# Expert rows weighted on chip and added to x1 in DRAM by accumulating scatters

## What is computed

```python
# layer 1: token mixing with a decaying scan over time, then residual and layer norm
xk, xv, xr = (x * m + shifted(x) * (1 - m) for m in (mix_k, mix_v, mix_r))
k, v, r = xk @ Wk.T, xv @ Wv.T, xr @ Wr.T
x1 = layernorm(x + (sigmoid(r) * wkv(decay, first, k, v)) @ Wo.T)

# layer 2: 8 experts, the best two of each token
logits = x1 @ Wg + bg
topk_scores, topk_idx = top_k(logits, 2)
topk_scores = softmax(topk_scores)
h = x1 @ W1[e] + b1[e];  a = gelu(h) if e is even else silu(h)
y[e] = a @ W2[e] + b2[e]
out = layernorm(x1 + sum over the two experts of topk_scores * y[e])
```

## Time and profile before

| | us |
|---|---|
| median of 3 runs (733.85 to 735.19) | 734.34 |
| the profiled execution, its own time | 729.4 |
| its span, first to last instruction | 727.4 |

### The profile page before, as it was taken

One profiled execution on the slowest core, in us unless ns is written; L12 is line 12 of the kernel. 1 busy time (PEld: TensorE's weight loads), 2 busy tenths in 40 slices (PEclk: granted clock), 3 DMA queues, 4 the chain that ended last, 5 costly groups with the idle time before them and its releaser, 6 DMA issues.

```text
span 727.4 us, 14812 instructions
## 1 busy us (share of the span) xinstructions
PE 639.8 (88%) x4525; PEld 591.6 (81%) x4525; DVE 461.5 (63%) x963; ACT 392.5 (54%) x715; POOL 304.7 (42%) x353
## 2 busy tenths in 40 slices
PE   8999999999876789999999999999999999996000
PEld 5887878878654689999999999999999999996000
DVE  4869999999996485574554654455534543432694
ACT  3576587568742244563636364665645455551474
POOL 5111044744665673191461722542821821112363
PEclk9999999999987799999999999999999999999555
DMA  8510232232317648514151142141231121100893
GB/s 258 135 30 15 73 110 96 86 102 81 108 60 232 197 153 277 184 51 151 37 167 40 43 161 61 35 161 51 76 131 41 29 60 46 31 28 32 285 299 117
DMA packets 57116, 78.75 MB, mean 108 GB/s; under 512 B 5190, under 2 KB 46611, under 8 KB 56884
## 3 DMA queue, kind: packets, MB, share of 16 engines
q1 hardware_dynamic: 41540, 51.59, 22.1%
q0 software_dynamic: 6496, 16.99, 6.6%
q10 hardware_dynamic: 8976, 8.72, 4.5%
HBM read 49.14 MB, written 28.92 MB: 107 GB/s over the span
## 4 chain that ended last, share of the span: by engine, by line
PE 72%; DVE 9%; issue 6%; POOL 4%; ACT 3%; DMA 3%; another core or an unknown queue 1%; SPq 0%; ACTq 0%; DVEq 0%; POOLq 0%
PE hT_ps L897 28%; PE y_ps L906 26%; PE vr_ps L734 6%; PE k_ps L734 5%; PE xT_ps L915 2%; PE wo_ps L742 2%; POOL records_dram L639 2%; DVE o_all L1245 1%; PE small_ps L756 1%; DMA recs<-records_dram 1%; PE xT_ps L725 1%; POOL rstd_c L693 1%; PE xT_ps L804 1%; ACT res L1163 1%
## 5 line engine op out<-in xcount | busy, mean ns | idle before, releaser
L897 PE MATMUL hT_ps<-xTh,wx 128*128 128x256 f32 x1120 | 212.3, 287 | 2.1 <-DVE aTl L1217 1.4
L906 PE MATMUL y_ps<-wx,aTh 128*128 128x256 f32 x1088 | 197.5, 283 | 1.1 <-DVE y_sb L1231 1.1
L897 PEld LDWEIGHTS hT_ps<-xTh,wx 128*128 128x128 f32 x1120 | 178.7, 193 | 2.8 <-DVE aTl L1217 1.6
L906 PEld LDWEIGHTS y_ps<-wx,aTh 128*128 128x128 f32 x1088 | 169.7, 192 | 1.3 <-issue 1.3
L674 POOL DMA_INDIRECT expert_out_dram<-y_sb,dest x70 | 68.3, 975 | 243.0 <-DVE y_sb L1231 227.4
L1217 DVE TENSOR_TENSOR aTl<-hT_ps,aTh 128x512 fp32r<-128x512 f32 x140 | 93.1, 688 | 118.0 <-ACT aTh L1108 114.6
L897 PE MATMUL hT_ps<-xTl,wx 128*128 128x256 f32 x560 | 159.3, 285 | 0.0
L906 PE MATMUL y_ps<-wx,aTl 128*128 128x256 f32 x544 | 154.0, 283 | 0.0
L1102 ACT ACT_TABLE_LOAD x33 | 42.3, 1283 | 170.3 <-PE hT_ps L897 163.4
L1102 ACT ACTIVATE hT_ps<-hT_ps,b_c 128x256 f32<-128x256 f32 x280 | 113.4, 467 | 20.0 <-DVE dest L1210 13.1
L897 PEld LDWEIGHTS hT_ps<-xTl,wx 128*128 128x128 f32 x560 | 108.5, 194 | 0.0
(11 more groups left out here) (201 smaller groups left out, 860.0 us busy)
## 6 DMA issues: line engine op xcount, KB each, us to landing
staging<-in_L_ffn_W SPq DMA_DIRECT2D x16, 1024.0 KB
recs<-records_dram ACTq DMA_DIRECT2D x33, 258.0 KB, 2.8
yy<-expert_out_dram SPq DMA_DIRECT2D x16, 512.0 KB, 5.5
xin<-in_L_attn_x SPq DMA_DIRECT2D x16, 256.0 KB, 4.4
xres<-in_L_attn_x SPq DMA_DIRECT2D x16, 256.0 KB, 3.2
x_dram<-rec SPq DMA_DIRECT2D x16, 256.0 KB
xx<-x_dram SPq DMA_DIRECT2D x2, 2048.0 KB
out<-res SPq DMA_DIRECT2D x16, 256.0 KB, 4.2
```

The source lines that it names most:

```text
L897: ins = pe.matmul(hT_ps[b][:, f, :], wx[:, s, part, off:off + P], xpart[t.slot % 2][:, cc, :], start=k == 0, stop=k == len(terms) - 1)
L906: ins = pe.matmul(y_ps[h], apart[t.slot % 2][:, fc, h * P:(h + 1) * P], wx[:, s, part, off:off + C], start=k == 0, stop=k == len(terms) - 1)
```

## The change

Each expert row is weighted on chip before it leaves, and added to its token's x1 row in DRAM. No separate tensor of expert rows exists any more.

- **Weights in the chunks.** `choose` writes the difference of the two scores (`gap`) in place of the copy `top2`. A new ACT function `weigh(c)` makes both weights, sigmoid(-gap) and sigmoid(gap), in columns C+3 and C+4 of the record. It stands before `exponents(i)` for chunk i-3 in the steps 3 to 7, and later for the last three chunks (after `normalise_x1(6)`, before `normalise_x1(7)`, and at the very end). The record now has 261 words instead of 258: x1, token number, both slots, both weights. The whole score calculation between the stages is gone. POOL's `send_records` also waits for `weigh`.
- **Blocks.** The row number is now the token number. `halves` no longer computes it; a new DVE function `mark` copies it and finds each record's weight in four small instructions, and stands after `lower_parts`. `outputs` adds the bias in place in PSUM, waits, then multiplies by the weight into `y_sb`: two instructions for each half in place of one.
- **Scatters.** POOL's indirect DMA writes into `x1_dram` with `compute_op=ALU.add`. Before the first half of block t it waits until both scatters of block t-1 have landed.
- **Last stage.** `xx`, `yy`, `y2`, `res` and their loads and sums are gone. SP issues eight loads (`zz`), each four tokens to a partition, 4 KB in one piece and 512 KB in all; DVE takes the statistics of four tiles, POOL makes four scales and shifts, ACT normalises in place, SP stores 512 KB.

The diff, cut to its core:

```diff
-    REC = C + 2
+    REC = C + 5
...
-    ys = nc.dram_tensor("expert_out_dram", (2 * TOKENS, C), F32, kind="Internal").ap()
+    sums = x1d.rearrange("b t c -> (b t) c")
...
-                if e == 2:
-                    for b in range(B):
-                        sp.dma_start(xx[:, :, b, :], x1d[b].rearrange("(q p) c -> p q c", p=P)).then_inc(xx_in, 16)
...
+            for g in range(GROUPS):
+                sp.dma_start(zz_of(g), rows_of(x1d, g)).then_inc(zz_in[g], 16)
+            for g in range(GROUPS):
+                sp.wait_ge(c_res, TILE * (g + 1))
+                sp.dma_start(rows_of(out, g), zz_of(g)).then_inc(res_out, 16)
...
+                pool.wait_ge(weighed, c.upto(2))
...
+                    previous = t - 1
                     for h in range(BH):
                         pool.wait_ge(y_done, t.upto(BH, h + 1))
+                        if h == 0 and previous.exists:
+                            pool.wait_ge(y_out[previous.slot], previous.turn(16 * BH, 16 * BH))
                         take_wait(pool)
                         pool.indirect_dma_start(
-                            ys, bass.IndirectOffsetOnAxis(ap=dest[t.slot][:, h:h + 1], axis=0), y_sb[t.slot][:, h, :], None,
-                            bounds_check=2 * TOKENS - 1, oob_is_err=False).then_inc(y_out[t.slot], 16)
+                            sums, bass.IndirectOffsetOnAxis(ap=dest[t.slot][:, h:h + 1], axis=0), y_sb[t.slot][:, h, :], None,
+                            bounds_check=TOKENS - 1, oob_is_err=False, compute_op=ALU.add).then_inc(y_out[t.slot], 16)
...
+            def weigh(c):
+                at = c.number % RECS
+                act.wait_ge(gap_done, c.upto(1))
+                scattered(act, c)
+                act.activation(rec[at][:, :, C + 3], gap[:], ACT.Sigmoid, scale=-1.0).then_inc(weighed, 1)
+                act.activation(rec[at][:, :, C + 4], gap[:], ACT.Sigmoid).then_inc(weighed, 1)
...
+                if (i - 3).exists and i.number < NCH:
+                    weigh(i - 3)
                 if i.exists:
                     exponents(i)
...
-            act.wait_ge(score_done, 1)
-            act.activation(score_t[:, :, 0:1], score_t[:, :, 0:1], ACT.Exp).then_inc(exp_done, 1)
...
+            for g in range(GROUPS):
+                act.wait_ge(c_rstd, g + 1)
+                for n in range(TILE):
+                    act.activation(zz_of(g)[:, n, :], zz_of(g)[:, n, :], ACT.Identity, bias=shift_c[:, g, n:n + 1],
+                                   scale=rstd_c[:, g, n:n + 1]).then_inc(c_res, 1)
...
+            def mark(u, own):
+                n = u.slot % 2
+                rows = recs[u.slot]
+                after(dve, y_out[u.slot], u.turn(16 * BH))
+                dve.tensor_copy(dest[u.slot][:], rows[:, :, C]).then_inc(dest_done, 1)
+                dve.tensor_tensor(hit[n][:], rows[:, :, C + 1:C + 3], own.rearrange("p a h -> p h a").broadcast_to([P, BH, 2]),
+                                  ALU.is_equal).then_inc(hit_done, 1)
...
+                dve.tensor_reduce(weight[u.slot][:], hit[n][:], AX.X, ALU.add).then_inc(weight_done, 1)
...
-                    dve.tensor_tensor(y_sb[u.slot][:, h, :], y_ps[h], b2_b[:, bass.ds(expert * C, C)],
-                                      ALU.add).then_inc(y_done, 1)
+                    dve.tensor_tensor(y_ps[h], y_ps[h], b2_b[:, bass.ds(expert * C, C)], ALU.add).then_inc(bias_added, 1)
+                    dve.wait_ge(bias_added, u.upto(BH, h + 1))
+                    dve.tensor_scalar(y_sb[u.slot][:, h, :], y_ps[h], weight[u.slot][:, h:h + 1], None, ALU.mult).then_inc(y_done, 1)
...
-                dve.tensor_copy(top2[:].rearrange("p i j k -> p (i j k)")[:, bass.ds(c.number * (2 * J), 2 * J)].rearrange(
-                    "p (j k) -> p j k", j=J), m8[:, :, 0:2]).then_inc(top2_done, 1)
+                after(dve, weighed, (c - 1).upto(2))
+                dve.tensor_tensor(gap[:], m8[:, :, 1], m8[:, :, 0], ALU.subtract).then_inc(gap_done, 1)
```

More of the change, by code:

```diff
@@ L204, in build @@
         m8 = sb("m8", [P, J, 8], F32, phase_a)
+        gap = sb("gap", [P, J], F32, phase_a)
         i8 = sb("i8", [P, J, 8], U32, phase_a)
@@ L254, in build @@
         dest = [sb(f"dest{n}", [P, BH], I32, phase_b) for n in range(RING)]
+        hit = [sb(f"hit{n}", [P, BH, 2], F32, phase_b) for n in range(2)]
+        weight = [sb(f"weight{n}", [P, BH], F32, phase_b) for n in range(RING)]
         xTh = [sb(f"xTh{n}", [P, CC, BLK], F32R, phase_b) for n in range(2)]
@@ L314, in build @@
         mm2_done, y_done = [sem(f"mm2_done{n}") for n in range(BH)], sem("y_done")
[L315 to L319, removed]
+        hit_done, weight_done, bias_added = sem("hit_done"), sem("weight_done"), sem("bias_added")
+        zz_in = [sem(f"zz_in{n}") for n in range(GROUPS)]
+        res_out = sem("res_out")
+        c_bn, c_mv, c_var, c_rstd, c_res = (sem(n) for n in ("c_bn", "c_mv", "c_var", "c_rstd", "c_res"))
         REC_DMAS = 2 * J * 16
@@ L355, in if_used, with rows_of, zz_of @@
             return eng.If(used > u.number) if u.largest >= ALWAYS else nullcontext()
[L357 to L368, removed]
+        def rows_of(ap, g):
+            b, q = g // (GROUPS // B), g % (GROUPS // B) * TILE
+            return ap[b].rearrange("(p q) c -> p q c", q=TILES)[:, q:q + TILE, :]
+        def zz_of(g):
+            b, q = g // (GROUPS // B), g % (GROUPS // B) * TILE
+            return zz[:, b, q:q + TILE, :]
         def after(eng, semaphore, value):
@@ L1491, in block_step @@
                         lower_parts(u)
+                u = t + 2
+                if u.exists:
+                    with if_used(dve, used, u):
+                        mark(u, own_f[:, bass.ds(u.number, 1)])
             blocks(dve, block_step)
-            dve.wait_ge(xx_in, 16 * B)
-            flat = score[:].rearrange("p n k -> p (n k)")
-            def first_sum(i):
-                dve.wait_ge(yy_in[i.slot], i.turn(16, 16))
-                after(dve, c_res, (i - RING).upto(B))
-                for b in range(B):
-                    dve.scalar_tensor_tensor(
-                        out=zz[i.slot][:, b, :], in0=yy[i.slot][:, b, 0:C], scalar=flat[:, bass.ds(column(i, b, 0), 1)],
-                        in1=xx[:, bass.ds(i.number, 1), b, :].rearrange("p a c -> p (a c)"),
-                        op0=ALU.mult, op1=ALU.add).then_inc(c_sum, 1)
@@ L1528, in out_step @@
-            def out_step(i):
-                for stage, c in ((first_sum, i), (statistics, i - 1), (second_sum, i), (means, i - 1)):
-                    if c.exists:
-                        stage(c)
-            pieces(dve, out_step)
-            last = Step(None, PIECES - 1, RING, PIECES)
-            statistics(last)
-            means(last)
+            for g in range(GROUPS):
+                dve.wait_ge(zz_in[g], 16)
+                for n in range(TILE):
+                    dve.bn_stats(stats_c[:, g, n, :], zz_of(g)[:, n, :]).then_inc(c_bn, 1)
+                dve.wait_ge(c_bn, TILE * (g + 1))
+                for n in range(TILE):
+                    dve.bn_aggr(mv_c[:, g, n, :], stats_c[:, g, n, :]).then_inc(c_mv, 1)
```

160 lines of the change are left out of this document (49 added, 111 removed).

## The result

| | before | after |
|---|---|---|
| median | 734.4 us (733.9 to 735.2) | 704.2 us (703.5 to 706.5) |
| profiled span | 727.4 us | 701.5 us |
| ratio | | 0.959 (95%: 0.957 to 0.962) |

What follows compares the result with a forecast made beforehand. It took DVE and PE, nearly full, to bound the chunks, PE the blocks, DMA with DVE the last stage. 7.3 + 1.0 + 1.5 - 22.2 = -12.4 us off 734.3 gave 721.9 us, range 711 to 733.

Steps and rivals of the forecast that it cites:

- Chunks, +7.3: Chunks: table loads for `weigh` delay the Exp on B by 3.1 us in steps 3 to 7, costing 7.3 us in sum.
- the loop: Chunks: dependence over two chunks, DVE to PE to ACT to DVE, as tight as DVE's own list; residual slack 2.2 us.
- Rivals 2 and 3: Chunks: table loads cost nothing, 714.6 us, 14%; or their full price in every chunk, 730.1 us, 12%.
- the drain: Chunks: the skill's 1.38 us added to each table switch, loop cost about 17 us, total near 731; chance 3%.
- Between the stages, 0: Between chunks and blocks: DVE's score instructions and the 4 MB load of x1 go, but PE waits for neither; nothing gained.
- Blocks, nothing: Blocks: added DVE work, about 1.5 us a block, and POOL's scatter waits fit beside PE's 11.94 us; no cost.
- Accumulating scatter, +1.5: End of the blocks: the last adding scatter lands later, 1.5 us, about half of an upper bound of 2.8.
- Rival 1: Blocks: the accumulating scatter becomes the bound; at 1 us a row about 934 us; chance 8%.
- Outputs, +1.0: End of the blocks: each output has one more instruction and wait, about 0.5 us, delaying PE's last product and the last scatter.
- Last stage, -22.2: Last stage: with half the loads it takes 31.2 us in place of 53.4, ACT setting the pace.
- Rival 4: Last stage: in-place tiles and 512 KB stores at the old pace leave 45 us or more, total 735 or above; 3%.
- From the span to the median, +4.9: Whole kernel: runs' median lay 4.9 us above the profiled execution; the same difference was assumed after the change.

Runs made afterwards that it cites:

- e4: Changed kernel with `weigh` of the first five chunks moved behind the upper halves, where Sigmoid is already loaded: 693.0 us, ratio 0.951 to the kernel before.
- e10: Changed kernel with `weigh` moved, operand distance 192, and `mark` of block 3 behind block 1's outputs: 692.8 us, ratio 0.944 to the kernel before.
- e1: Kernel before plus an unused 320-byte tile ahead of `recs`, giving the changed kernel's operand distance: 716.3 us, ratio 0.982.
- e3: Changed kernel plus two unused tiles restoring the operand places of the kernel before (distance 0): 711.9 us, ratio 0.976 to the kernel before.
- e5: Not the layer: only a block's products on constant operands, places swept in 32-byte steps; 48 first plus 48 second products took 10.90 to 11.52 us.
- e6: Changed kernel with plain scatters in place of accumulating ones (addition left out): 699.8 us, ratio 0.960 to the kernel before.
- e12: Kernel before plus an unused 192-byte tile ahead of `recs`, operand distance 192 in place of 0: 716.6 us, ratio 0.985.
- e2: Kernel before plus unused tiles of 1280 bytes ahead of staging and 320 ahead of `recs`, giving the changed kernel's operand places: 717.2 us, ratio 0.982.

## Why the prediction was right and wrong

- *Chunks, +7.3*: right in the mechanism, which e4 shows, since the loop was followed through both engines. That the sum agrees to the tenth is luck: chunk 7 cost 1.3 in place of 0.2, and chunks 4 and 6 each 0.5 less than worked out. Rivals 2 and 3 and the drain fall with it. What the prediction didn't ask is whether `weigh` could stand at a place in ACT's list where Sigmoid is loaded anyway; e4 shows that it can.
- *Between the stages, 0*: 1.8 us. e10 removes 1.3 of it: `mark` stands ahead of outputs for which PE waits in the first blocks, before the steady state whose slack the prediction used. The other 0.5 was not followed and is within what this stretch varies by.
- *Blocks, nothing*: here the step failed. The prediction went through DVE's and POOL's new work and found that PE waits for none of it, which is true from block 3 on. From that it put the stage at nothing, and so took the time of PE's own instructions as unchanged, for which it gave no reason. "The PE distance between blocks still 11.94" was the test set for it, and it read 11.55 to 11.75. e1 to e3 and e5 show the cause: the tiles moved by a few hundred bytes. That accounts for 9.2 of the 13.5 us by which the span was missed (10.2 to 10.7 us between like kernels at distances 0 and 64), and by the ratios of e1 and e3 for 12 to 13 us in the medians, 3 either way, of a miss of 18. This gain is luck: nothing in the idea of the change asks for it.
- *Accumulating scatter, +1.5*: mis-sized, 0.2 to 0.4 us by e6 and hidden by a shorter last group of products (5.74 against 6.02 us in the earlier trace rows). Half of an upper bound is no measurement. The Trainium skill ("Collectives: The Full Stack", The bandwidth ceiling) gives the halved pace of an adding transfer for large collectives in a ring. It is not seen in this scatter of 128 rows: 3.52 to 3.72 us with the addition against 3.32 without it in e6. Rival 1 falls.
- *Outputs, +1.0*: right, twice 0.5.
- *Last stage, -22.2*: -26.3. The mechanism was right up to the last store (ACT unbroken, 16 us). The wrong term is the tail, 3.8 us in place of 6.2 + 0.8: the 6.2 was taken for the time of a store, but the store landed after 2.1 and the end waited for POOL's DRAIN. By an estimate (727.4 - 723.3 before, 701.5 - 701.2 after) about 4 us of this stage's gain are that DRAIN, which no longer ends last, and not the lesser work. Rival 4 falls.
- *From the span to the median, +4.9*: the profiled execution of the kernel before lay 4.9 us below its median, and the prediction carried that over. After the change it was 0.7, so 4.2 us of the miss of 18 are this term. In which stage the slower executions lose them, no trace shows.
- *The range*: with every bound of the change's own terms it held the change at equal places (17 us, 15 to 20, so 717). It had no term for what it left untouched.

## What to carry to other kernels

A change in a tile's size or number moves every tile behind it, so compare the time of untouched instructions first (here 48 products, 5.75 us before and 5.46 or 5.66 after), and repeat the change once with padding that restores the old places before its gain is credited to its idea. Where PE is the bound, sweep the distance between its two operands in SBUF by itself; an unused tile of 128 to 320 bytes was worth 6 to 13 us here. Then time the kernel itself at the best places, for its own groups did not follow the sweep throughout (e12). And before the time behind a last store is called the store's, look for what ended last. An activation with another table should stand where that table is loaded anyway: in ACT's list, look for the last user of the same table ahead of the point where the value is needed.

## What the runs showed of the hardware that was not expected

- The pace of fp32r products of 256 columns depends on the distance modulo 256 bytes between the places of their two operands in SBUF: 48 of them take from 5.44 us (192) to 5.76 us (0), with nothing else running. The granted clock is 1.00 at either. The absolute place made no difference (wx moved by 1280 bytes from e1 to e2, by 32 in e5).
- An accumulating indirect scatter of 128 rows of 1 KB holds POOL for 1.55 us, the plain one for 0.98; its landing is 0.2 to 0.4 us longer (e6).
- POOL's DRAIN at the end takes 7.2 to 7.4 us in the five kernels with plain indirect scatters and 4.5 in the eight with accumulating ones. Its cause is open.
- In steady state a group at the same distance can take 5.45 or 5.66 us; at distance 192 the pattern returns every four blocks. Its cause is open.
